# Gated pass of a four-layer graph network: node sums taken in column groups of TensorE, two batches at a time

## The reference, cut to what matters

```python
msg_in = concatenate([h[src], h[dst], e], axis=-1)            # 128 + 128 + 64
messages = silu(msg_in @ w1 + b1) @ w2 + b2
gates = sigmoid(msg_in @ wg + bg)
messages = messages * gates
agg = segment_sum(messages, dst, n)
deg = segment_sum(ones(E), dst, n)
agg = agg / maximum(deg, 1.0)[:, None]
h_new = silu(concatenate([h, agg], axis=-1) @ wu + bu)
x = layernorm(x + h_new)
```

## Time and profile before

| what | value |
|---|---|
| median of three runs | 1939.49 us |
| the profiled execution, its own time | 1941.41 us |
| its span, first to last instruction | 1939.5 us |
| gated pass, first `add_pre` to last count added | 70.0 to 657.2 us |
[...]
| PE busy in the whole span | 84% |
| DVE, ACT, POOL busy | 75%, 54%, 48% |

### The profile page before, as it was taken

One profiled execution on the slowest core, in us unless ns is written; L12 is line 12 of the kernel. 1 busy time (PEld: TensorE's weight loads), 2 busy tenths in 40 slices (PEclk: granted clock), 3 DMA queues, 4 the chain that ended last, 5 costly groups with the idle time before them and its releaser, 6 DMA issues. The chain is left out here.

```text
span 1939.5 us, 44470 instructions
## 1 busy us (share of the span) xinstructions
PE 1623.6 (84%) x13670; PEld 1310.2 (68%) x13670; DVE 1463.3 (75%) x4393; ACT 1049.4 (54%) x2866; POOL 937.0 (48%) x940
## 2 busy tenths in 40 slices
PE   6699999999999749998556988956588887499996
PEld 5588888888887616556455877856477777266664
DVE  5688888888887698996668888856888886644656
ACT  2577677776776366773306878830377785311000
POOL 4777777777776120000455777535667773200000
PEclk9799999999999859999755999976589998699998
DMA  6888788888887002333552111127121112254442
GB/s 197 251 268 244 243 261 245 258 264 259 260 247 238 11 5 80 126 126 126 161 111 53 42 41 42 36 62 193 40 59 40 42 41 86 86 194 173 171 170 91
DMA packets 148931, 273.61 MB, mean 141 GB/s; under 512 B 28039, under 2 KB 88909, under 8 KB 146436
## 3 DMA queue, kind: packets, MB, share of 16 engines
q1 hardware_dynamic: 110430, 192.44, 30.3%
q0 software_dynamic: 33408, 75.68, 14.6%
q10 hardware_dynamic: 4854, 2.55, 0.5%
HBM read 225.06 MB, written 45.51 MB: 140 GB/s over the span
## 5 line engine op out<-in xcount | busy, mean ns | idle before, releaser
L997 POOL DMA_INDIRECT gated_rows<-p_tab,src_idx x416 | 436.8, 1050 | 150.3 <-issue 124.9
L1405 POOL DMA_INDIRECT cur<-table,src_idx x240 | 245.3, 1022 | 105.9 <-issue 49.4
L2260 PE MATMUL bank<-counts,mean_xs 128*128 128x416 bf16 (+2 forms) x1350 | 220.4, 322 | 32.0 <-DVE mean_xs L1762 32.0
L1593 PE MATMUL bank<-attention_counts,h_sb 128*128 128x260 f32 (+1 forms) x900 | 216.4, 363 | 13.8 <-ACT attention_counts L1548 9.9
L1526 ACT ACTIVATE attention_lo<-attention_plain,w_left 128x128 fp32r<-128x128 bf16 x512 | 176.7, 394 | 87.1 <-DVE attention_plain L1640 87.0
L1038 PE MATMUL bank<-gated_wide_q,gated_comb 128*128 128x256 f32 x832 | 216.0, 382 | 0.0
L1114 ACT ACTIVATE gated_sig<-gated_pre 128x512 f32<-128x512 f32 x208 | 131.4, 632 | 152.9 <-DVE gated_pre L1202 145.6
L2260 PEld LDWEIGHTS bank<-counts,mean_xs 128*128 128x128 bf16 x1350 | 126.4, 98 | 116.8 <-issue 35.4
L1202 DVE TENSOR_TENSOR gated_pre<-bank,gated_rows 128x512 f32<-128x512 f32 x208 | 142.8, 687 | 79.3 <-PE bank L1038 79.3
L1576 PE MATMUL bank<-attention_wide_a,attention_lo 128*128 128x300 f32 x512 | 151.7, 380 | 46.0 <-issue 31.8
L1593 PEld LDWEIGHTS bank<-attention_counts,h_sb 128*128 128x128 f32 x900 | 146.8, 191 | 26.2 <-ACT attention_counts L1548 17.4
(11 more groups left out here) (450 smaller groups left out, 3983.2 us busy)
## 6 DMA issues: line engine op xcount, KB each, us to landing
counts<-count_tabs SPq DMA_DIRECT2D x16, 2675.0 KB, 9.8
h_sb<-in_edge_attr_dram SPq DMA_DIRECT2D x51, 512.0 KB
count_tabs<-mean_counts SPq DMA_DIRECT2D x40, 535.0 KB, 2.7
gated_relr<-rel_rows SPq DMA_DIRECT2D x104, 128.0 KB
gated_ids<-id_rows SPq DMA_DIRECT2D x26, 512.0 KB
gated_wide_q<-q_tab SPq DMA_DIRECT2D x208, 64.0 KB
attend_hot_lo<-low_hots SPq DMA_DIRECT2D x52, 256.0 KB
gated_ea<-in_edge_attr_dram SPq DMA_DIRECT2D x51, 256.0 KB
```

Source lines behind the costliest of these rows:

```text
L997: pool.indirect_dma_start(out=rows[:, q % TICKS, c, :], out_offset=None, in_=p_tab, in_offset=bass.IndirectOffsetOnAxis(ap=src_idx[:, b, j ...
L1405: pool.indirect_dma_start(out=ring_row(n, j), out_offset=None, in_=table, in_offset=bass.IndirectOffsetOnAxis(ap=src_idx[:, gathered_batch ...
L1593: mm = pe.matmul(BANKS_D[k % 2][:, 0:width], h_sb[:, m, :], counts[:, home(first), m, at:at + width], start=(m == 0), stop=(m == NT - 1), ...
L2260: mm = pe.matmul(BANKS_D[q % ND][:, 0:width], xs[l][:, m // 3, m % 3, :], counts[:, s % 2, m // 3, at:at + width], start=(m == 0), stop=(m ...
```

## The change

Messages and one-hots change places. `hot` is now stationary, 32 of its 64 columns at a time, and the messages move with a 129th column of ones, so that one matmul gives 32 nodes by 128 features and their counts. The four column groups take chunk parity and half of the window (`at = c*W + h*W//2`), so the 128 partitions of `SEG` hold two partial sums of 64 nodes. Two batches (four pairs, LUMP = 4) are summed in one go, ahead of the transposes of every fourth step, directly behind the edge terms, which now also come for two batches at once. ACT lifts the 258 columns into `lump` (`lift`), and two steps later PE multiplies `lump` by two stacked 64 by 64 identities (`fold`): this adds the two halves and turns the sum to features by nodes, 128 columns stationary; the ones column is folded by a second matmul whose stationary operand is that one column. DVE adds both batches in the step behind. `halve_hot` and `hot_b` go; the ring of messages has 8 pairs and that of turned features 8. `w_c` and `w_left`, which the profile and the lists name, are memory lent to `lump` and `fold`.

```diff
-                    def sum_up(q):
-                        b, k, u = batch(q)
-                        pe.wait_ge(msg_ready, q + 1)
...
-                        for c in range(2):
-                            j = 2 * k + c
-                            pe.matmul(SEG[b % 2][:, 0:W], msg[:, q % 2, c, :], hot[:, u, j, :],
-                                      start=(j == 0), stop=(j == J - 1), skip_group_check=True)
-                        for c in range(2):
-                            j = 2 * k + c
-                            mm = pe.matmul(SEG[b % 2][:, W:2 * W], ones_b[:, :], hot_b[:, u, j, :],
-                                           start=False, stop=(j == J - 1), skip_group_check=True)
-                        mm.then_inc(summed, 1)
+                    def sum_up(g):
+                        pe.wait_ge(msg_ready, (g + 1) * LUMP)
+                        pe.wait_ge(hot_ready, (g + 1) * 2)
+                        reach(pe, lifted, g)
+                        for i in range(2):
+                            for k in range(PAIRS):
+                                q = g * LUMP + i * PAIRS + k
+                                for c in range(2):
+                                    for h in range(2):
+                                        at = c * W + h * W // 2
+                                        mm = pe.matmul(SEG[at:at + W // 2, i * (P + 1):(i + 1) * (P + 1)],
+                                                       hot[:, (2 * g + i) % UN, 2 * k + c, h * W // 2:(h + 1) * W // 2], msg[:, q % MSL, c, :],
+                                                       start=(k == 0), stop=(k == PAIRS - 1), skip_group_check=True)
+                        mm.then_inc(summed, 1)
+
+                    def fold_up(g):
+                        pe.wait_ge(lifted, g + 1)
+                        reach(pe, added, 2 * g)
+                        for i in range(2):
+                            pe.matmul(FOLD[:, i * W:(i + 1) * W], lump[:, i, 0:P], fold[:, :], start=True, stop=True)
+                            mm = pe.matmul(FOLD[0:1, (2 + i) * W:(3 + i) * W], lump[:, i, P:P + 1], fold[:, :], start=True, stop=True)
+                        mm.then_inc(folded, 1)
...
-                        if k == PAIRS - 1:
-                            for j in range(J):
-                                pe.matmul(ST[j * AE_COLS:(j + 1) * AE_COLS, 2 * P:3 * P], ae_v[:, :], eaT[:, (q - k + j // 2) % TRN, j % 2, :],
-                                          start=True, stop=True, skip_group_check=True)
+                        if (q + 1) % (TERMS * PAIRS) == 0:
+                            for i in range(TERMS):
+                                for j in range(J):
+                                    pe.matmul(ST[j * AE_COLS:(j + 1) * AE_COLS, (2 + i) * P:(3 + i) * P], ae_v[:, :],
+                                              eaT[:, (q + 1 - (TERMS - i) * PAIRS + j // 2) % TRN, j % 2, :],
+                                              start=True, stop=True, skip_group_check=True)
+                        if (q + 1) % LUMP == 0 and q >= LUMP:
+                            sum_up(q // LUMP - 1)
...
-                            act.copy(ae_rows[:, b // AG_ % 2, b % AG_, :], ST[:, 2 * P:3 * P]).then_inc(ae_placed, 1)
+                            first = b % AG_ + 1 - TERMS
+                            act.copy(flat(ae_rows[:, b // AG_ % 2, first:first + TERMS, :]), ST[:, 2 * P:(2 + TERMS) * P]).then_inc(ae_placed, 1)
...
-                    def halve_hot(b):
-                        act.wait_ge(hot_ready, b + 1)
-                        reach(act, summed, (b - UN + 1) * PAIRS)
-                        act.copy(hot_b[:, b % UN, :, :], hot[:, b % UN, :, :]).then_inc(hot_b_ready, 1)
+                    def lift(g):
+                        act.wait_ge(summed, g + 1)
+                        reach(act, folded, g)
+                        act.copy(flat(lump[:, :, :]), SEG[:, 0:2 * (P + 1)]).then_inc(lifted, 1)
...
+                    dve.memset(msg[:, :, :, P:P + 1], 1.0).then_inc(ready, 1)
+                    for half in (low, high):
+                        dve.tensor_copy(fold[half, :], ident[half, half]).then_inc(ready, 1)
...
-                            if 0 <= i - 7 < NQ and (i - 7) % PAIRS == PAIRS - 1:
-                                b = (i - 7) // PAIRS
+                            if i >= ADD_AT and (i - ADD_AT) % LUMP == 0:
+                                b = (i - ADD_AT) // LUMP * 2
                                 if b % 8 == 0:
                                     values = loaded_starts(mybir.EngineType.DVE, base[0:1, b:b + 8])
                                 add(b, values[b % 8])
+                                add(b + 1, values[(b + 1) % 8])
```

More of the change, by code:

```diff
@@ L848, in gated_pass @@
             comb, wide_q = sb("comb", [P, UN, PAIRS, 2, P]), sb("wide_q", [P, UN, 2, 2 * P])
-            hot, hot_b = sb("hot", [P, UN, J, W]), sb("hot_b", [P, UN, J, W], BF16)
-            TRN = 6
+            hot = sb("hot", [P, UN, J, W])
+            LUMP = 2 * PAIRS
+            MSL, NGR = 2 * LUMP, NB * PAIRS // LUMP
+            lump = flat(w_c[:, :, :])[:, 0:2 * (P + 1)].rearrange("p (b d) -> p b d", b=2)
+            fold = flat(w_left[:, :, :])[:, 0:W]
+            assert NB % 2 == 0 and UN >= 4
+            TRN, TERMS = 8, 2
             ea128 = flat(h_sb[:, :, :])[:, J * P:J * P + UN * J * P].rearrange("p (b j d) -> p b j d", b=UN, j=J)
@@ L855, in gated_pass @@
             AG_ = 4
+            assert AG_ % TERMS == 0 and NB % AG_ == 0
             ae_rows = sb("ae_rows", [P, 2, AG_, P])
@@ L859, in gated_pass @@
             pre, sig = sb("pre", [P, 2, 2, 2 * P]), sb("sig", [P, 4, 2, 2 * P])
-            silu, siluT, msg = sb("silu", [P, 2, 2, P]), sb("siluT", [P, 2, 2, P]), sb("msg", [P, 2, 2, P])
+            silu, siluT, msg = sb("silu", [P, 2, 2, P]), sb("siluT", [P, 2, 2, P]), sb("msg", [P, MSL, 2, P + 1])
             ids, low_hot = sb("ids", [P, 2, LG * BE], BF16), sb("low_hot", [P, 2, LG * BE], F8)
@@ L881, in gated_pass @@
             per_round = [*self_sems, ae_placed, *ae_kept, *ids_in, *looks_kept, looks_made, *ea64_in, *ea128_in, *relr_in, *q_in, ea_turned, made, s_turned, m_made, summed, eaT_ready, sig_ready, sT_ready,
-                         hot_b_ready, pre_ready, silu_ready, msg_ready, hot_ready, hotT_ready, added]
+                         lifted, folded, pre_ready, silu_ready, msg_ready, hot_ready, hotT_ready, added]
             PRE = [bank[0], bank[1]]
-            SEG = [bank[2], bank[3]]
+            SEG, FOLD = bank[2], bank[3]
             EAT, ST, M = bank[4], bank[5], bank[6]
@@ L888, in gated_pass @@
             BACK = UN * PAIRS
+            LIFT_AT, FOLD_AT, ADD_AT = 11, 13, 14
             def batch(q):
@@ L948, in keep_edge_terms @@
                     def keep_edge_terms(g):
-                        sp.wait_ge(ae_placed, (g + 1) * AG_)
+                        sp.wait_ge(ae_placed, (g + 1) * AG_ // TERMS)
                         for l in range(2):
@@ L1005, in _ @@
                     pe.wait_ge(loaded, 16 * 6)
-                    pe.wait_ge(ready, 3)
+                    pe.wait_ge(ready, 6)
                     pe.wait_ge(split, 5 + 6)
@@ L1062, in make_msg @@
                         mm.then_inc(m_made, 1)
-                    def sum_up(q):
-                        b, k, u = batch(q)
-                        pe.wait_ge(msg_ready, q + 1)
[L1067 to L1070, removed]
-                        for c in range(2):
-                            j = 2 * k + c
-                            pe.matmul(SEG[b % 2][:, 0:W], msg[:, q % 2, c, :], hot[:, u, j, :],
-                                      start=(j == 0), stop=(j == J - 1), skip_group_check=True)
-                        for c in range(2):
-                            j = 2 * k + c
-                            mm = pe.matmul(SEG[b % 2][:, W:2 * W], ones_b[:, :], hot_b[:, u, j, :],
-                                           start=False, stop=(j == J - 1), skip_group_check=True)
-                        mm.then_inc(summed, 1)
                     with rounds_of(pe) as rr:
-                        for i in range(NQ + 6):
+                        for i in range(NQ + 10):
                             if i in SELF_AT:
@@ L1094, in _ @@
                                 make_msg(i - 5)
-                            if 0 <= i - 6 < NQ:
-                                sum_up(i - 6)
-                        pe.wait_ge(summed, NQ)
+                            if i - 4 == NQ + LUMP - 1:
+                                sum_up(NGR - 1)
+                            if i >= FOLD_AT and (i - FOLD_AT) % LUMP == 0:
+                                fold_up((i - FOLD_AT) // LUMP)
+                        pe.wait_ge(folded, NGR)
                         next_round(pe, rr)
@@ L1141, in _ @@
                     with rounds_of(act) as rr:
-                        for i in range(NQ + 5):
+                        for i in range(NQ + 9):
```

(16 more changed lines are left out.)

8 lines of the change are left out of this document (4 added, 4 removed).

## The result

The changed kernel takes 1945.32 us (median of six runs, 1945.05 to 1947.44) against 1938.64 us for the kernel before in the same sessions; the ratio is 1.0037, interval 1.0024 to 1.0050. It is slower by 0.4%, 6.7 us, where 10.5 was forecast. The profiled execution spans 1943.3 us.

A forecast was written before the change was run, and what follows sets the result against it. PE was taken to bound the pass. Terms -1 + 2 + 9 + 0.3 + 1 = +11 us on the profiled 1941.4 gave 1952, a median of 1950 us; own range 1941 to 1958, 8 in 10 from 1926 to 1966.

The forecast's parts named there:

- PE bounds the pass: From 120 to 620 us PE, busy 497 of 500 us, sets the pace; POOL stands close behind.
- What goes, 2.00 us left in a step: PE loses sums (1.80 us) and two edge-term excursions (1.02) per four pairs; 8.00 stays, four steps of 2.00.
- The large excursion 1.61 us: PE's sums and edge terms in column groups: 12 waves of 0.11 us plus the excursion's own 0.29.
- the rival of unhidden loads: Weight loads in a column group are not hidden: large excursion 1.88 us, total 1960 us; chance 0.15.
- The fold 1.19 us: PE's fold per four pairs: wide matmuls 0.39, one-column matmuls 0.22, two excursions of 0.29 us each.
- The rival without it: The one-column matmul does not leave the full array's mode: fold 0.61 us, total 1930 us; chance 0.13.
- PE's sum, -1 us: PE's four pairs take 8.00 + 1.61 + 1.19 = 10.80 us against 10.82, over 52 groups -1 us.
- The looks, +9 us: Second add and wider copy around DVE's looks make PE lose 0.25 to 0.55 us more, 26 times; 9 taken.
- Plain steps, +2 us: PE asks for the turned silu's bank 0.45 us earlier: 0 to 0.1 us in 104 plain steps, 2 taken.
- the rival of steps paced by DVE and ACT: Each of 104 plain steps loses over 0.1 us to the add_pre, sigmoid, silu copy chain: 1965 us; chance 0.12.
- the rival in which the stalls go: The longer excursion step absorbs the looks, saving today's 9 us of stalls: total 1931 us; chance 0.15.
- The ends, +1.3 us: Three small DVE instructions ahead of the loop cost 0.3 us; last sums, lift, fold and adds net 1 us.

The follow-up runs named there:

- counts together: Changed kernel with the fold's four matmuls ordered wide, wide, one column, one column instead of alternating: ratio 0.9973 to the kernel before.
- looks in pieces: DVE's long look quartered over odd steps, mask at end of step 1, on four kernels: changed 0.9916, before 0.9965, edge terms merged 0.9896, wide counts 0.9864.
- wide counts: Changed kernel with ones column first and counts folded by 128 stationary columns, not one: ratio 0.9984 to the kernel before.
- wide counts with pieces: Changed kernel with counts folded by 128 stationary columns and DVE's looks in five pieces: 1915.11 us, ratio 0.9864 to the kernel before.
- the adds moved: Changed kernel with a group's two DVE adds two steps later (ADD_AT 16 for 14), looks left in place: ratio 0.9996 to the kernel before.

## Why the prediction was right

The forecast was 1950 us, slower; the time is 1945.3. Point by point:

- *PE bounds the pass*: confirmed. With the looks out of the way the time follows PE's steps.
- *What goes, 2.00 us left in a step*: 1.97 to 2.02.
- *The large excursion 1.61 us*: 3.57 - 1.97 = 1.60, and 1.69 in its dearer form. Waves follow each other by 0.11 us, so weight loads hide and the rival of unhidden loads falls. Its quarter of a load was an estimate that no run shows: a load of 32 columns is open for 0.11 us (L1059), one of 128 for 0.14 (L1085) to 0.19 (L1094). The own price of an excursion, 0.29, was measured at 0.30.
- *The fold 1.19 us*: 1.05 (3.02 - 1.97), so the forecast was 0.14 too dear: the own price of its two excursions was taken from the edge terms, 0.29 each, where counts together gave 0.23. That a one-column matmul costs what L1048 did was the author's estimate, and no run shows it. An excursion of its own for each one-column matmul that stands between full ones was shown twice (made wide, a fold took 0.85 us for 1.03; put together, 0.80). The rival without it falls.
- *PE's sum, -1 us*: mis-sized. With looks in pieces, eight steps go from 21.65 to 21.27, 26 times 0.38, -10 us. 0.14 in each of 52 folds is 7 of these.
- *The looks, +9 us*: mis-sized the other way. They cost 0.34 us in eight steps before (21.99 - 21.65) and 1.00 after (22.27 - 21.27): 26 x 0.66 = 17 us, where 0.35 was taken. The totals say the same: pieces gain 24 us on the changed kernel and 7 on the one before. The chain was right link by link; the second add cost more than its 0.39 (0.54 us more from `gate_msg` to the look: 396.91 - 395.78, against 306.32 - 305.72), and the 0.2 at EAT came nearly in full.
- *Plain steps, +2 us*: none without a look; the rival of steps paced by DVE and ACT falls. So does the rival in which the stalls go.
- *The ends, +1.3 us*: held. From the last first-transpose to the pass's end are 18.9 us for 14.9, and from the last `gate_msg` (661.06) to the last count (665.58) 4.5 us, where about 4 were forecast. But most of this is work on PE that the eight steps count already. The pass ends 8.4 us later, 26 x 0.28 = 7.3 of it by the steps, which leaves 1.1 for both ends.
- *Behind the pass* nothing was forecast. The span grew by 3.8 us where the pass grew by 8.4. The rest of the execution, from the pass's end, lasts 1277.1 to 1283.4 us in the fourteen profiles, 1281.9 before and 1277.3 after, with no order among the kernels that the edits would explain. Why it varies wasn't tested; for totals the medians decide, not single profiles.

Two errors of size, -9 and +8, met each other; that 1950 was so near is in part luck.

Of the signs that the prediction named, two were badly chosen. The rows of L1059 and L1079 last 1.06 and 0.64 us, about midway to the 1.2 and beyond the 0.55 of the rival of the loads. But their records overlap, each open for 0.27 to 0.30 us with the next wave 0.11 behind it; by starts the two take 0.88 (eight waves of 0.11) and 0.46 us, close to the 0.9 and 0.45 forecast. And no idle time ahead of L1069 is listed: its loads start 0.07 us behind the end of those ahead of them and the next ones 0.12 behind its own, shorter than the gaps that the profile lists (0.15 and more). The experiments settle what these signs left open.

Where the gain went is shown by a row of kernels with looks in pieces: 21.65 us in eight steps before, 21.07 with the edge terms merged, 21.27 with the sums in column groups and one-column counts as well, 20.78 with wide counts. Merging edge terms is the gain (-0.58, -15 us; 13 by the ratios). The swap of operands by itself costs 0.20, because two of its three excursions hold one column each; with these gone it gains 0.29. These two are read from step times; in the totals they are +4 us, inside the intervals, and -6 us, just outside. Then the looks, untouched by the edit, took 17 us.

## What to carry to other kernels

Count changes between the full array and column groups, beside the matmuls: an excursion had a price of its own, 0.28 to 0.30 us with two, four or twelve waves in it and 0.23 for one-column matmuls. A matmul of one stationary column between full ones was such an excursion, and 128 columns were cheaper (a fold of 0.85 us for 1.03). When steps become uneven or shorter, look at the longest rare instruction of the engine behind, and follow the chain from it to the next bank that must be free; cutting it into pieces freed the steps of all four kernels, while moving it helped only where the sums were swapped (16 us of 24 in the changed kernel), since idle time ahead of an instruction is no room if its chain has no slack. A merge that gains can hide a rewrite that loses: time them apart.

## What the runs showed of the hardware

A gather of GpSimd that ran beside the long look took over twice as long as the others. GpSimd's timeline in the changed kernel, where the long look runs from 396.91 to 398.18:

```profile
395.69 0.99 POOL L1004 DMA_INDIRECT gated_rows<-p_tab,src_idx  x1 [0.30 <-issue]
396.98 2.50 POOL L1004 DMA_INDIRECT gated_rows<-p_tab,src_idx  x1 [0.30 <-issue]
399.79 0.95 POOL L1004 DMA_INDIRECT gated_rows<-p_tab,src_idx  x1 [0.31 <-issue]
```

From 120 to 620 us the 23 gathers that overlap a long look last 2.2 us in the mean and the others 0.98; before the change it was 2.3 and 0.97. With looks in pieces the 92 that overlap a piece last 0.95, as the others do. GpSimd's rows, changed kernel, then with looks in pieces:

```profile
L1004 POOL DMA_INDIRECT gated_rows<-p_tab,src_idx x357 | 378.5, 1060 | 123.9 <-issue 97.7 <-DVE gated_pre L1225 26.2
```
```profile
L1004 POOL DMA_INDIRECT gated_rows<-p_tab,src_idx x363 | 345.9, 953 | 142.3 <-issue 73.0 <-DVE gated_pre L1231 69.2
```

The mean fell from 1060 to 953 ns with the same gathers. The cut is not the only way there: with the adds moved and the look whole it was 988, and the 45 gathers that overlap a look there last 1.26 us in the mean for 2.2, so it also matters when the look begins. The floor of 10.6 us for four pairs, which the prediction took from the earlier trace rows, was no floor, since these long gathers were in it: in wide counts with pieces the same sum gives 350.8 us busy and 92.2 of issue for 181 pairs, 9.8 us for four, and four pairs take 20.78 / 2 = 10.4 us by medians. And the one-column matmul and the one-column transposes behaved differently: the transposes of the earlier trace rows follow at 0.09 us, L1069 only after 0.2.
